# The light stage's loops over tiles, written out for every engine with constant waits and fixed addresses

## The chip, the cores and the metric

The kernel runs on one core of a Trainium2 chip. The metric is the device time of one execution in microseconds. A core has five engines with instruction streams of their own: TensorE (PE; its weight loads are listed apart as PEld), VectorE (DVE), ScalarE (ACT), GpSimd (POOL) and SyncE (SP). They meet through semaphores: an instruction adds to one when it is done, and another waits until it has reached a value.

## What is computed

Sixteen sequences of 512 tokens with 128 channels pass through a block of transformer layers: a feed-forward layer with routing, a latent attention, the same feed-forward layer again, an expert layer, a cosine attention and the expert layer again. The change lies in the light branch of the feed-forward layer, which runs twice. In the reference:

```python
def light_local_attn(x, gamma, wq, wkv, wo):
    xn = rmsnorm(x, gamma)
    q = xn @ wq
    k, v = jnp.split(xn @ wkv, 2, axis=-1)
    # windows of WIN = 128 tokens, HEADS = 8 heads of DH = 64
    q, k, v = (win(q) * SCALE, win(k), win(v))
    attn = jax.nn.softmax(jnp.einsum('bwhid,bwhjd->bwhij', q, k), axis=-1)
    out = jnp.einsum('bwhij,bwhjd->bwhid', attn, v)
    return out.transpose(0, 1, 3, 2, 4).reshape(b, n, HID) @ wo

def coor_descent(s, k):            # 50 rounds for the router, on scores of all tokens
    def body(_, ab):
        a, b = ab
        a = EPS * (logk - logsumexp((s + b) / EPS, axis=-1, keepdims=True))
        b = -relu(s + a)
        return (a, b)
    ...
```

The router then takes the 128 and the 256 tokens with the highest scores of each sequence (`top_k`).

## The kernel before

The 8192 tokens are 64 tiles of 128 tokens, one window each. `light_attention` (L346) runs them through a pipeline: five engines each have a `body(i, u, d, r)` that is called once for every pass i from -1 to 66. In pass i different tiles are at different steps. "Tile i" in this document means pass i. TensorE projects q and k of tile i (L507), does the output projection of tile i-3 (L514), transposes the probabilities of tile i-2 (L522), projects v (L527), transposes the input of tile i+1 (L532), makes the scores (L540) and multiplies probabilities and values of tile i-2 (L565). A pass begins with the first weight load of L507, and cuts are made there.

VectorE in a pass: row maxima `mx` of the scores (L653), the scores minus these, `ssub` (L657), half a round of the descent (`settle` L647, `descend` L641 and L642), `y` = the output plus the residual (L666), row sums `rsum` of the probabilities (L671), their reciprocals `rec` (L675), the normalised input of a later tile, `xr` (L632), and another half round. ScalarE: `oT` (L590), exponential `prob` (L595, needs `ssub`), `qkT` (L600), exponential and logarithm of the descent (L581, L583), `probT` (L606, twice), `v` (L609), `xrT` (L612) and the descent once more. GpSimd multiplies the probabilities by `rec` in two halves (L478). The order on an engine is the order in `body`, written by hand; nothing schedules it.

The passes 3 to 27 carry the descent (argument d), 28 to 59 the selection of the highest scores on VectorE (argument r; `max` L689, `match_replace` L692; `xr` is made on ScalarE there, L576), the others neither. `windows` (L416) calls `body` for the passes: -1 to 3 written out, 4 to 27 in a loop of six rounds of four passes (L421), 28 to 31 written out, 32 to 43 (L426) and 44 to 59 (L430) in loops of three and four rounds, 60 to 66 written out. `between(1)` and `between(2)` do work once after passes 43 and 59, on VectorE a mask of the selected tokens (L726, L729). In a loop, i is a register: a wait such as `dve.wait_ge(rec_ready, i)` compares with a register that has to be computed, and `x[:, bass.ds(j, 1), :]` is an address that has to be computed.

The stage is called with tag `f1l` (first call, 50 to 530 us of the span) and `f2l` (second call, from 1540 us).

Of the kernel before, what the change touches and what calls it, by code (L numbers as in the profile page):

```python
# [19 lines left out]
NT = TOK // P  # L20
# [325 lines left out]
def light_attention(nc, tag, x, y, scale_a, shift_b, s_rows, smax, na, logk, posw, wparts, lw, hw, w, ident, weff=None, consts=None):  # L346
# [5 lines left out]
    VB = 4  # L352
    wqkv, wo = lw["wqkv"], lw["wo"]
    with ExitStack() as ctx:
# [56 lines left out]
        D0 = 3  # L411
        D1 = D0 + ITERS // 2
        RQ, RKV = NQ // 8, NKV // 8
        E0 = D1 + RKV

        def windows(eng, body, between):  # L416


            for i in range(-1, VB):
                body(i, i % VB, 0 if i == D0 else None, None)  # L420
            with eng.Fori(1, D1 // VB) as k:  # L421
                for u in range(VB):
                    body(VB * k + u, u, 2 * (VB * k) + 2 * (u - D0) - 1, None)
            for i in range(D1, D1 + VB):
                body(i, i % VB, None, i - D1)
            with eng.Fori(D1 // VB + 1, (D1 + RQ) // VB) as k:  # L426
                for u in range(VB):
                    body(VB * k + u, u, None, VB * k + u - D1)
            between(1)
            with eng.Fori((D1 + RQ) // VB, E0 // VB) as k:  # L430
                for u in range(VB):
                    body(VB * k + u, u, None, VB * k + u - D1)
            between(2)
            for i in range(E0, NT + 3):
                body(i, i % VB, None, None)

        def live(i, lag=0):
            return not isinstance(i, int) or 0 <= i - lag < NT
# [27 lines left out]
        @block.gpsimd  # L466
        def _(pool):
            nc.gpsimd.memset(ones[:], 1.0).then_inc(filled, 1)
            if weff is not None:
                nc.gpsimd.memset(weff[:, 3:5], 0.0).then_inc(turned_clear, 1)  # L470

            def body(i, u, d, r):
                if live(i, 1):
                    pool.wait_ge(rec_ready, i)
                    pr, rc = prob[(u - 1) % 2], rec[(u - 1) % 2]
                    for n in range(2):
                        g = slice(PAIRS * n, PAIRS * n + PAIRS)
                        nc.gpsimd.tensor_tensor(pr[:, g], pr[:, g],  # L478
                                                rc[:, g].rearrange("p (h o) -> p h o", o=1).broadcast_to([P, PAIRS, P]),
                                                ALU.mult).then_inc(norm_ready, 1)  # L480

            def between(n):
                if n == 1:
                    pool.wait_ge(scores_ready, 1)
                    nc.gpsimd.tensor_scalar(one_minus[:], scores[:], -1.0, 1.0, ALU.mult, ALU.add).then_inc(less_ready, 1)
                    pool.wait_ge(less_ready, 1)
                    nc.gpsimd.tensor_tensor(weight[:], scores[:], one_minus[:], ALU.add).then_inc(weight_ready, 1)
                if n == 2:
                    pool.wait_ge(hw_in, 64)
                    kv = hraw[:, HID:3 * HID].rearrange("p (h s d) -> p s h d", h=HEADS, s=2)  # L490
                    nc.gpsimd.tensor_scalar(hw["wq"][:], hraw[:, 0:HID], hgamma[:, 0:1], None, ALU.mult)
                    nc.gpsimd.tensor_scalar(hw["wk"][:].rearrange("p (h d) -> p h d", h=HEADS), kv[:, 0], hgamma[:, 0:1], None, ALU.mult)
                    nc.gpsimd.tensor_scalar(hw["wv"][:].rearrange("p (h d) -> p h d", h=HEADS), kv[:, 1], hgamma[:, 0:1], None, ALU.mult)

            windows(pool, body, between)

        @block.tensor
        def _(pe):

            def body(i, u, d, r):  # L500
# [58 lines left out]
                if live(i, 2):  # L559
# [7 lines left out]
                    last.then_inc(o_ps, 1)  # L567

            windows(pe, body, lambda n: None)

        @block.scalar
        def _(act):
# [12 lines left out]
            def body(i, u, d, r):  # L585
# [35 lines left out]
                if at(i, NT + 2) and weff is not None:  # L621
                    act.wait_ge(weff_ps, 1)
                    nc.scalar.copy(weff[:, 0:3], ps_s[:, 0, 0:3]).then_inc(weff_sb, 1)

            windows(act, body, lambda n: None)

        @block.vector
# [2077 lines left out]
```

## Time and profile before

| what | value |
|---|---|
| median of three runs | 3093.97 us (3090.47 to 3094.25) |
| span of the profiled execution | 3097.8 us |
| busy share PE, DVE, ACT, POOL | 88%, 75%, 59%, 51% |
| tiles 4 to 27, first call / second call | 184.40 us / 187.58 us |
| tiles 32 to 59, first call / second call | 192.62 us / 192.72 us |

The span is the time from the first to the last instruction of one execution that was taken with the profiler; it lies 3.8 us above the median of the runs without it. The light stage is about 0.95 ms of it. The granted clock of TensorE is 1.00, its upper level of 2.4 GHz, over all tiles from 3 on in both calls. Register, branch and semaphore instructions are not counted as busy time, and the views do not list them: they show as idle time before the next instruction.

### The profile page before, as it was taken

How to read it: one execution, taken by the hardware profiler on the slowest of the kernel's cores; microseconds unless marked ns; L12 is line 12 of the kernel's file. 1: busy time of each engine (PE TensorE's matmuls, PEld its weight loads, DVE VectorE, ACT ScalarE, POOL GpSimd, SP SyncE). 2: the span in 40 equal slices, each digit the busy share in tenths (PEclk: the TensorE clock that was granted, in tenths of full speed). 3: DMA queues.
4: the chain of work that ended last, by engine and by line, in shares of the span. 5: the costliest groups of instructions: out<-in, count | busy, mean ns of one | idle time of the engine just before them, and what ended most of it. 6: DMA issues, size and time to landing. Idle time of an engine off the chain costs nothing. (4 is left out here: it accounts for less than half of the span.)

```text
span 3097.8 us, 73081 instructions
## 1 busy us (share of the span) xinstructions
PE 2738.8 (88%) x24470; PEld 1839.9 (59%) x24470; DVE 2312.9 (75%) x6119; ACT 1827.4 (59%) x3759; POOL 1587.2 (51%) x1866
## 2 busy tenths in 40 slices
PE   7989998999589999999788899989988469999795
PEld 4777887687223333333377788868766335555663
DVE  5898776788488888888388877779976357777563
ACT  3777665555246666666577766645553148876531
POOL 1222323787446666765322233377755646564446
PEclk9999999999779999999899999999988659999797
DMA  4000000000223333332000000000044365654343
GB/s 114 3 0 1 0 1 1 1 0 0 75 66 81 84 76 80 75 84 63 15 1 0 1 1 1 1 1 0 0 102 126 57 158 143 147 141 120 93 141 40
DMA packets 156192, 161.99 MB, mean 52 GB/s; under 512 B 42064, under 2 KB 134480, under 8 KB 155344
## 3 DMA queue, kind: packets, MB, share of 16 engines
q1 hardware_dynamic: 146624, 150.97, 19.3%
q0 software_dynamic: 9216, 7.87, 2.0%
q8 instruction: 113, 1.85, 0.3%
q14 instruction: 95, 0.78, 0.1%
q10 hardware_dynamic: 144, 0.52, 0.1%
HBM read 83.37 MB, written 74.87 MB: 51 GB/s over the span
## 5 line engine op out<-in xcount | busy, mean ns | idle before, releaser
L1969 DVE CUSTOM_DVE_ANT_0 la_ps<-la_ps,la_tri 128x512 f32<-128x512 f32 (+3 forms) x1024 | 481.8, 514 | 100.1 <-PE la_ps L1496 92.7
L1773 ACT ACTIVATE la_prob<-la_ps 128x512 f32<-128x512 f32 x640 | 373.8, 601 | 247.5 <-PE la_ps L1507 240.7
L478 POOL TENSOR_TENSOR f2l_prob<-f2l_prob,f2l_rec 128x512 f32<-128x512 f32 x128 | 133.1, 1060 | 330.8 <-DVE f2l_rec L675 330.8
L478 POOL TENSOR_TENSOR f1l_prob<-f1l_prob,f1l_rec 128x512 f32<-128x512 f32 x128 | 133.0, 1060 | 327.0 <-DVE f1l_rec L675 327.0
L1496 PE MATMUL la_ps<-la_ks,la_qs 48*128 48x512 bf16 (+3 forms) x1024 | 259.1, 321 | 45.0 <-DVE la_mx L1969 28.0
L1363 POOL TENSOR_SCALAR_AFFINE_SELECT la_prob<-la_prob 128x512 f32<-128x512 f32 x256 | 159.4, 634 | 217.6 <-ACT la_prob L1773 217.3
L1507 PE MATMUL la_ps<-la_qs,la_ks 50*128 50x512 bf16 (+3 forms) x1024 | 244.4, 310 | 5.8 <-ACT la_prob L1773 2.0
L1967 DVE TENSOR_REDUCE ca_mx<-ca_ps 128x4 f32<-128x512 f32 x256 | 174.2, 687 | 96.5 <-PE ca_ps L1496 95.5
L1507 PEld LDWEIGHTS la_ps<-la_qs,la_ks 50*128 50x128 bf16 x1024 | 67.0, 94 | 235.4 <-ACT la_prob L1773 162.9
L1773 ACT ACTIVATE ca_prob<-ca_ps 128x512 f32<-128x512 f32 x256 | 152.1, 602 | 89.4 <-PE ca_ps L1507 89.2
L1539 PE MATMUL la_ps_o<-la_prob,la_v 128*32 128x512 f32 (+3 forms) x2048 | 199.8, 464 | 0.0
L1969 DVE DVE_READ_ACCUMULATOR2_ANT la_mx<- 128x1 f32 x1024 | 144.6, 141 | 0.0
L1496 PEld LDWEIGHTS la_ps<-la_ks,la_qs 48*128 48x128 bf16 x1024 | 67.2, 95 | 113.7 <-DVE la_mx L1969 91.5
L507 PE MATMUL f2l_ps_qk<-f2l_xrT,fw_wqkv 128*128 128x128 f32 x1024 | 133.0, 284 | 0.7 <-ACT f2l_xrT L612 0.7
L507 PE MATMUL f1l_ps_qk<-f1l_xrT,fw_wqkv 128*128 128x128 f32 x1024 | 133.0, 284 | 0.7 <-ACT f1l_xrT L612 0.7
L507 PEld LDWEIGHTS f2l_ps_qk<-f2l_xrT,fw_wqkv 128*128 128x128 f32 x1024 | 120.7, 194 | 11.7 <-issue 10.5
L507 PEld LDWEIGHTS f1l_ps_qk<-f1l_xrT,fw_wqkv 128*128 128x128 f32 x1024 | 120.7, 194 | 11.7 <-issue 10.4
L595 ACT ACTIVATE f2l_prob<-f2l_ssub 128x1024 f32<-128x1024 f32 x64 | 67.8, 1059 | 85.2 <-DVE f2l_ssub L657 82.5
L595 ACT ACTIVATE f1l_prob<-f1l_ssub 128x1024 f32<-128x1024 f32 x64 | 67.7, 1059 | 79.5 <-DVE f1l_ssub L657 79.5
L1496 PE MATMUL ca_ps<-ca_ks,ca_qs 56*128 56x128 bf16 x1024 | 100.8, 228 | 10.7 <-DMA ca_ks<-stack_image 6.0
L1507 PE MATMUL ca_ps<-ca_qs,ca_ks 58*128 58x128 bf16 x1024 | 99.7, 224 | 3.2 <-ACT ca_prob L1773 1.9
L1507 PEld LDWEIGHTS ca_ps<-ca_qs,ca_ks 58*128 58x128 bf16 x1024 | 58.7, 96 | 69.4 <-ACT ca_prob L1773 35.6
(541 smaller groups left out, 8013.0 us busy)
## 6 DMA issues: line engine op xcount, KB each, us to landing
stack_image<-la_parts SPq DMA_DIRECT2D x192, 128.0 KB, 2.4
stack_image<-ca_parts SPq DMA_DIRECT2D x192, 128.0 KB, 2.4
la_qs<-stack_image SPq DMA_DIRECT2D x64, 192.0 KB, 3.5
la_ks<-stack_image SPq DMA_DIRECT2D x64, 192.0 KB, 4.3
ca_qs<-stack_image SPq DMA_DIRECT2D x64, 192.0 KB, 3.4
ca_ks<-stack_image SPq DMA_DIRECT2D x64, 192.0 KB, 4.3
gather_table<-fw_wqkv SPq DMA_DIRECT2D x16, 256.0 KB, 2.3
gather_table<-m_pr SPq DMA_DIRECT2D x32, 128.0 KB, 2.2
```

What stands on the lines that cost most here:

```text
L478: nc.gpsimd.tensor_tensor(pr[:, g], pr[:, g], rc[:, g].rearrange("p (h o) -> p h o", o=1).broadcast_to([P, PAIRS, P]), ALU.mult).then_inc( ...
L507: last = nc.tensor.matmul(ps_qk[:, t, p], wqkv[:, t, p * P:(p + 1) * P], xrT[:], start=True, stop=True)
L595: nc.scalar.activation(prob[(u - 1) % 2][:], ssub[:], ACT.Exp, scale=SM).then_inc(p_sb, 1)
L1363: return nc.gpsimd.affine_select(view, view, pattern=[[0, 4], [1, P]], compare_op=ALU.is_ge, fill=0.0, base=0, channel_multiplier=-1)
L1496: last = nc.tensor.matmul(bank[:, col:col + width], qs[u][rows, h // 2, qblk * P:(qblk + 1) * P], ks[u][rows, h // 2, keys], start=True, s ...
L1507: last = nc.tensor.matmul(bank[:, col:col + width], ks[u][rows, h // 2, blk * P:(blk + 1) * P], qs[u][rows, h // 2, blk * P:blk * P + widt ...
L1539: last = nc.tensor.matmul(ps_o[32 * j:32 * j + 32, blk * P:T], v[u][:, blk, 4 * q + j, :], prob[q % 2][:, unit, col:col + width], start=bl ...
L1773: nc.scalar.activation(prob[q % 2][:, n], ps2[n % 2][:], ACT.Exp, scale=SM).then_inc(S["p_sb"], 1)
L1967: last = nc.vector.tensor_reduce(m, bank[:].rearrange("p (a b) -> p a b", a=TPB), X_AX, ALU.max)
L1969: last = nc.vector.tensor_tensor_reduce(bank[:, col:col + width], bank[:, col:col + width], tri[:, T - width:T], 1.0, -BIG, ALU.add, ALU.m ...
```

## The change

`windows` no longer makes loops. It calls `body` with plain numbers for every pass, so that every wait has a constant and every address is fixed. The order of the calls, the arguments and the places of `between` are the same.

```diff
-            for i in range(-1, VB):
-                body(i, i % VB, 0 if i == D0 else None, None)
-            with eng.Fori(1, D1 // VB) as k:
-                for u in range(VB):
-                    body(VB * k + u, u, 2 * (VB * k) + 2 * (u - D0) - 1, None)
-            for i in range(D1, D1 + VB):
-                body(i, i % VB, None, i - D1)
-            with eng.Fori(D1 // VB + 1, (D1 + RQ) // VB) as k:
-                for u in range(VB):
-                    body(VB * k + u, u, None, VB * k + u - D1)
-            between(1)
-            with eng.Fori((D1 + RQ) // VB, E0 // VB) as k:
-                for u in range(VB):
-                    body(VB * k + u, u, None, VB * k + u - D1)
-            between(2)
-            for i in range(E0, NT + 3):
-                body(i, i % VB, None, None)
+            for i in range(-1, NT + 3):
+                descent = max(0, 2 * (i - D0) - 1) if D0 <= i < D1 else None
+                body(i, i % VB, descent, i - D1 if D1 <= i < E0 else None)
+                if i == D1 + RQ - 1:
+                    between(1)
+                if i == E0 - 1:
+                    between(2)
```

The built programs show it engine by engine. VectorE, second call, in the first loop, from the end of a half round of the descent to `xr`; ISA and REGISTER_ALU rows are register arithmetic for waits and addresses. Before:

```order
L664 ISA
L666 ISA x2
L666 SCALAR_TENSOR_TENSOR g_x<-f2l_ps_a,g_y 128x128
L670 ISA
L671 TENSOR_REDUCE f2l_rsum<-f2l_prob 128x8
L672 ISA
L674 ISA
L675 RECIPROCAL f2l_rec<-f2l_rsum 128x8
L677 ISA
L632 ISA x2
L632 REGISTER_ALU
L632 SCALAR_TENSOR_TENSOR f2l_xr<-g_y,g_a,g_b 128x128
```

After (the lines of the changed file are ten lower), with the instruction ahead of it:

```order
L632 TENSOR_SCALAR f2l_tmin<-f_s_rows,f_na 48x512
L656 SCALAR_TENSOR_TENSOR g_x<-f2l_ps_a,g_y 128x128
L661 TENSOR_REDUCE f2l_rsum<-f2l_prob 128x8
L665 RECIPROCAL f2l_rec<-f2l_rsum 128x8
L622 SCALAR_TENSOR_TENSOR f2l_xr<-g_y,g_a,g_b 128x128
```

The four working instructions keep their order, and the register rows between them are gone.

ScalarE, second call, in the first loop, around the exponential of the probabilities. Before:

```order
L583 ACTIVATE f2l_lsum<-f2l_esum 48x1
L587 REGISTER_ALU
L589 ISA
L590 COPY f2l_oT<-f2l_ps_v 128x512
L592 ISA
L594 ISA
L595 ACTIVATE f2l_prob<-f2l_ssub 128x1024
L597 ISA
L599 ISA
L600 COPY f2l_qkT<-f2l_ps_qk 128x1024
```

After:

```order
L573 ACTIVATE f2l_lsum<-f2l_esum 48x1
L580 COPY f2l_oT<-f2l_ps_v 128x512
L585 ACTIVATE f2l_prob<-f2l_ssub 128x1024
L590 COPY f2l_qkT<-f2l_ps_qk 128x1024
L571 ACTIVATE f2l_eexp,f2l_esum<-f2l_tmin,f2l_nm 48x512
```

Here too the register rows are gone and the working instructions stand as they stood.

## Rows read from the trace of the kernel before

**Rows 1.** Stretch, length, busy us of PE, PEld, DVE, ACT, POOL; clock, DMA share, GB/s.

```profile
75.47:82.31 6.84, 6.84 (x70) 5.82 (x68) 5.23 (x8) 5.05 (x10) 2.16 (x3) 1.00 0.15 34
82.31:266.71 184.40, 165.71 (x1610) 140.27 (x1609) 167.75 (x289) 143.56 (x310) 50.02 (x48) 1.00 0.00 0
295.78:488.40 192.62, 191.56 (x1878) 162.88 (x1876) 151.32 (x226) 127.91 (x224) 58.90 (x58) 1.00 0.00 1
1566.47:1754.05 187.58, 166.00 (x1611) 139.66 (x1609) 163.70 (x289) 145.35 (x310) 50.04 (x48) 1.00 0.00 0
```

**Rows 2.** Waits, 113 to 258 us: total us, times, longest.

```profile
ACT f1l_prob L595 <- DVE f1l_ssub L657: 16.8, 19, 1.0
PE f1l_ps_v L565 <- ACT f1l_v L609: 14.1, 18, 0.9
```

**Rows 3.** Timeline, tiles 13 to 15: start, us, instruction, [idle before and its releaser].

```profile
153.35 1.06 PE L514 MATMUL f1l_ps_a<-fw_wo,f1l_oT 128*128 128x128 f32 x8
...
154.58 0.29 DVE L666 SCALAR_TENSOR_TENSOR g_y<-f1l_ps_a,g_x 128x128 f32 x1 [0.27 <-PE f1l_ps_a L514]
...
156.14 0.20 DVE L675 RECIPROCAL f1l_rec<-f1l_rsum 128x8 f32<-128x8 f32 x1
...
156.42 2.08 POOL L478 TENSOR_TENSOR f1l_prob<-f1l_prob,f1l_rec 128x512 f32<-128x512 f32 x2 [5.67 <-DVE f1l_rec L675]
156.44 1.17 DVE L632 SCALAR_TENSOR_TENSOR f1l_xr<-g_x,g_a,g_b 128x128 f32 x1
...
159.95 1.23 DVE L657 TENSOR_TENSOR f1l_ssub<-f1l_ps_s,f1l_mx 128x1024 f32<-128x1024 f32 x1
...
161.29 1.06 ACT L595 ACTIVATE f1l_prob<-f1l_ssub 128x1024 f32<-128x1024 f32 x1 [0.96 <-DVE f1l_ssub L657]
...
165.78 1.09 PE L565 MATMUL f1l_ps_v<-f1l_probT,f1l_v 128*64 128x128 f32 x16 [0.84 <-ACT f1l_v L609]
...
169.92 0.29 DVE L666 SCALAR_TENSOR_TENSOR g_y<-f1l_ps_a,g_x 128x128 f32 x1 [0.26 <-PE f1l_ps_a L514]
```

**Rows 4.** Timeline, tile 3, outside the loops.

```profile
75.36 1.22 DVE L657 TENSOR_TENSOR f1l_ssub<-f1l_ps_s,f1l_mx 128x1024 f32<-128x1024 f32 x1
...
76.62 1.06 ACT L595 ACTIVATE f1l_prob<-f1l_ssub 128x1024 f32<-128x1024 f32 x1 [0.46 <-DVE f1l_ssub L657]
...
77.36 1.06 PE L514 MATMUL f1l_ps_a<-fw_wo,f1l_oT 128*128 128x128 f32 x8
...
78.45 0.29 DVE L666 SCALAR_TENSOR_TENSOR g_y<-f1l_ps_a,g_x 128x128 f32<-128x128 f32 x1 [1.36 <-PE f1l_ps_a L514]
...
79.91 0.20 DVE L675 RECIPROCAL f1l_rec<-f1l_rsum 128x8 f32<-128x8 f32 x1
...
80.19 2.08 POOL L478 TENSOR_TENSOR f1l_prob<-f1l_prob,f1l_rec 128x512 f32<-128x512 f32 x2 [4.64 <-DVE f1l_rec L675]
...
80.30 1.08 DVE L632 SCALAR_TENSOR_TENSOR f1l_xr<-g_x,g_a,g_b 128x128 f32<-128x128 f32 x1 [0.19 <-PE f1l_ps_a L532]
```

**Rows 5.** Timeline, second call, tile 13.

```profile
1640.17 0.29 DVE L666 SCALAR_TENSOR_TENSOR g_x<-f2l_ps_a,g_y 128x128 f32 x1
...
1641.87 0.20 DVE L675 RECIPROCAL f2l_rec<-f2l_rsum 128x8 f32<-128x8 f32 x1 [0.17 <-DVE f2l_rsum L671]
```

**Rows 6.** Timeline, tile 1, outside the loops.

```profile
67.61 0.30 DVE L632 SCALAR_TENSOR_TENSOR f1l_xr<-g_x,g_a,g_b 128x128 f32<-128x128 f32 x1
67.78 2.04 POOL L478 TENSOR_TENSOR f1l_prob<-f1l_prob,f1l_rec 128x512 f32<-128x512 f32 x2 [12.09 <-DVE f1l_rec L675]
```

**Rows 7.** Transfers of 113 to 258 and 488 to 525 us; fetch queue; a group of the first attention.

```profile
DMA packets 0, 0.00 MB, mean 0 GB/s; under 512 B 0, under 2 KB 0, under 8 KB 0
...
DMA packets 3, 0.04 MB, mean 1 GB/s; under 512 B 0, under 2 KB 0, under 8 KB 0
...
q8 instruction: 113, 1.85, 0.3%
...
L1969 DVE CUSTOM_DVE_ANT_0 la_ps<-la_ps,la_tri 128x512 f32<-128x512 f32 (+3 forms) x1024 | 481.8, 514 | 100.1 <-PE la_ps L1496 92.7 <-issue 0.2
```

## The prediction

> **What bounds the kernel now.** I read the light stage first in the table of busy time by stretch, cut at the places where TensorE's first weight load of a tile (L507) begins [rows 1]. Tile 3 still stands outside any loop: 6.84 us long, PE busy for all of it. So 6.84 us is what a tile costs when PE never waits. Tiles 32 to 59 (two of the three loops, 28 tiles) take 192.62 us, or 6.88 us each, with PE busy 191.56 us: PE is the bound there too, and shorter code on other engines can win little. Tiles 4 to 27 (the first loop, 24 tiles, with the descent of the router on DVE and ACT) are another matter: 184.40 us in the first call, 7.683 us a tile, and 187.58 us in the second, 7.816 us a tile, although the work is the same. PE is busy for 165.71 and 166.00 us of these, VectorE for 167.75 and 163.70 us, or at most 6.99 us a tile. No engine is full, so a chain of waits sets the pace, and the second call's extra 0.13 us is not arithmetic.
>
> The list of waits names the chain [rows 2]: PE waits for `v` from ACT before L565, ACT waits for `ssub` from DVE before the exponential. The third link is in the timeline, where DVE's `y` (L666) sits idle until PE's L514 releases it. There I followed the chain through two tiles [rows 3]: `y` at 154.58; `rec` at 156.14 (1.56 later); `ssub` of the next tile ends at 159.95 + 1.23 = 161.18 (5.04 later; GpSimd's multiply at 156.42 and `xr` at 156.44 lie inside); ACT's exponential starts 161.29 (0.11); PE's L565 starts 165.78 (4.49); DVE's `y`, two tiles on, starts 169.92 (4.14). Sum 15.34 us for two tiles, 7.67 each: this chain is the measured 7.683.
>
> **The change part by part.** Same instructions, same order. What goes is branches, and the register arithmetic that puts a wait value or an address before an instruction. It counts only where its instruction was about to start, which is three places in the chain. For each, tile 3, already written with constants, gives the price after [rows 4].
> - Before `y`: in the loop `y` starts 154.58, while L514 ended at 153.35 + 1.06 = 154.41, so 0.17 us. In tile 3 L514 ended at 77.36 + 1.06 = 78.42 and `y` starts at 78.45, so 0.03. Link 4.14 becomes 4.00.
> - Before `rec`: 1.56 from `y` in the loop, 79.91 - 78.45 = 1.46 in tile 3. Gain 0.10.
> - Before the exponential: 0.11 in the loop; in tile 3 `ssub` ends at 75.36 + 1.22 = 76.58 and the exponential starts at 76.62, so 0.04. Gain 0.07.
>
> I leave the links 5.04 and 4.49 alone. Register work inside them runs under long operations (ACT goes without a gap from the exponential to `v`), and `xr`, which also loses address arithmetic, is held by something else: in the loop it starts 0.02 us after GpSimd's multiply and takes 1.17 us [rows 3], in tile 3 it starts 0.11 after it and takes 1.08 [rows 4], and both end 1.19 us after GpSimd began. In tile 1, ahead of GpSimd, it took 0.30 us [rows 6]. Whoever comes second waits for the first multiply, so an earlier `xr` behind GpSimd ends no earlier.
>
> Sum after: 1.46 + 5.04 + 0.04 + 4.49 + 4.00 = 15.03 us for two tiles, 7.515 each. DVE alone would allow less (6.99 busy) and PE 6.84, so the chain still binds, only shorter. First call: 24 x (7.683 - 7.515) = 4.0 us. Second call: its loop is slower by more register work, `y` to `rec` takes 1641.87 - 1640.17 = 1.70 us instead of 1.56 [rows 5]. Written out both calls run the same form, so I take 7.515 there too: 24 x (7.816 - 7.515) = 7.2 us. The bounds: if the second call came down only to the first call's present 7.683, 24 x 0.133 = 3.2 us; if all of it goes, 7.2. I take 7.2, because the programs of the two calls read alike after the change.
>
> Tiles 32 to 59: 192.62 - 28 x 6.84 = 1.1 us above PE's own pace. That contains the mask at the middle, which stays. Bounds 0 and 1.1 us in a call; I take the middle, 0.5, since the mask costs VectorE part of it, so 1.0 us for both. Branches (13 loop rounds a call on four engines) lie in these measured means and get no price of their own. The straight tiles, the other stages and all transfers are not touched: 0.
>
> Total 4.0 + 7.2 + 1.0 = 12.2 us. The profiled execution has a span of 3097.8 us and gives 3085.6. The median of the shown runs is 3.8 us lower at 3093.97, so 3093.97 - 12.2 = 3081.8: **3082 us**.
>
> **Rivals.**
> A. *`xr` gets ahead of GpSimd.* In tile 3 `xr` was released by PE's L532 and came 0.11 us too late [rows 4]. If DVE runs a little later against PE, so that `rec` and with it GpSimd start over 0.11 later, `xr` goes first and takes 0.30 us [rows 6] where it ended 1.19 us after GpSimd's start. That takes some 0.8 us out of the link of 5.04: 14.2 us for two tiles, 7.1 each, a further 48 x 0.41 = 20 us, so 3062; with PE's 6.84 as a floor, 3050. Against it: two such chains run interlocked, one through the even tiles and one through the odd. Where `y` starts as soon as L514 ends, as in the chain's own pace, GpSimd wins as in tile 3. A tile in which `y` comes late can flip, but its neighbour then has `y` on time and stays at 15.03 for two tiles, and the mean stays 7.515 with tiles alternately long and short. So I expect flips in every other tile at most. The Trainium skill (SBUF — State Buffer, Who interferes with whom) says that a VectorE instruction with two SBUF inputs and a GpSimd instruction that reads SBUF exclude each other, and that issue order decides who blocks. The durations 0.30, 1.08 and 1.17 agree. By that rule a shift of 0.11 us in issue order would be worth this rival's whole 20 us.
> B. *Nothing measurable.* The three gains are eaten by the next wait: `rec` or `y` is early, but the last releaser (`v`, the probabilities, GpSimd) is late by other causes. Full loss of the gain gives 3094; half of it 3088. For it: idle DVE time is small (7.683 - 6.99 = 0.69 us a tile), so there is not much to squeeze. Against: each of the three gaps ends directly at a link of the chain that adds up to 7.67 of 7.683.
> C. *Slower: the written-out code has to be fetched.* During the first loop the instruction queues are silent: no packet at all in 145 us. In a straight stretch of 37 us (5.4 tiles) there are 3 packets; instruction queue q8 moved 113 in 0.3% of 16 engines' 3097.8 us, or about 1.3 us each [rows 7]. Estimated from this, 52 tiles a call that leave the loops cost 29 packets, 58 for both calls. Shown outright on the path each would be 1.3 us: 76 us, 3158. From 9 exposed packets the gain is gone, from 14 on it is measurably slower. Against it: tile 3 is straight code at PE's full pace, and the first attention runs DVE straight through 1024 pairs of instructions with 0.2 of 100.1 us idle put down to issue [rows 7], so fetching is ahead of use. The Trainium skill (Runtime: NRT & Kernel Launch, Instruction fetch mechanics) says that streaming is mostly hidden, but that a taken branch to a target outside the fetched window forces a fetch. The silent queue shows that these loops' branches cause none, so the removal of branches wins nothing by that rule.
> D. *The change does not do what it says*, and register work remains: the order of instructions shows none on DVE in these tiles after the change. I give it no chance of its own.
>
> **How the numbers follow.** Forecast (3077 to 3087): 0.60. A (3050 to 3077): 0.13. B (3087 to 3095): 0.19. C (over 3095): 0.08. About 0.2%, 6 us, is what a measurement of this kernel can tell from no change; 3094 - 6 = 3088 divides faster from same. So faster 0.74 (the edge of B with it), same 0.18, slower 0.08. The range takes in the forecast, A down to its two-tile value 3062 and B up to 3092, where half of the gain and more is lost; it leaves out A's floor and C: 3062 to 3092.
>
> **What would show it.** In the profile after: tiles 4 to 27 take 180.4 us (24 x 7.515) in both calls, perhaps alternating; the two calls agree, where they now differ by 3.2 us. `y` starts 0.03 us after L514's end, or after its own `tmin`; `rec` 1.46 after `y`; the exponential 0.04 after `ssub`; `xr` still takes 1.0 us or more in at least every other tile. Tiles 32 to 59 take about 192.1 us. The forecast is wrong if `xr` takes 0.3 us in all tiles (A), if tiles 4 to 27 stay above 7.65 us (B), or if gaps stand on PE, ACT or DVE that no releaser explains and that come along with packets of the instruction queues (C).

## The result, and the profile after

The median falls from 3093.81 us to 3072.97 us (five runs of each; 3068.53 to 3089.76 after, 3085.86 to 3094.25 before). The ratio is 0.9939, with an interval from 0.9915 to 0.9964. In microseconds that is 20.8 less, and anything from 11.1 to 26.3 less is inside the interval (3093.81 x 0.0036 and x 0.0085). The profiled execution after has a span of 3088.0 us, where before had 3097.8. The four stretches below are cut as in [rows 1], at TensorE's first weight load of a tile, now L497: tiles 4 to 27 and 32 to 59 of the first call, then the same of the second. Columns: stretch, length, busy us of PE, PEld, DVE, ACT, POOL (with counts), granted clock, DMA share, GB/s.

```profile
81.93:262.03 180.10, 165.66 (x1610) 140.66 (x1608) 153.33 (x289) 143.79 (x310) 51.86 (x48) 1.00 0.01 2
291.05:482.91 191.86, 191.47 (x1879) 162.86 (x1877) 149.15 (x226) 130.24 (x224) 59.12 (x59) 1.00 0.01 1
1565.95:1746.05 180.10, 165.65 (x1610) 140.65 (x1608) 153.48 (x290) 144.17 (x312) 52.05 (x48) 1.00 0.01 2
1775.06:1966.92 191.86, 191.47 (x1878) 162.85 (x1876) 148.80 (x226) 130.34 (x224) 59.11 (x59) 1.00 0.01 2
```

Against [rows 1] the first loop has lost 4.30 us in the first call and 7.48 us in the second. The two calls took 184.40 and 187.58 us; now both take 180.10. Tiles 32 to 59 have lost 0.76 us in the first call and 0.86 in the second (192.62 and 192.72 before). That is 13.4 us in all. Of the gain in tiles 32 to 59, 0.56 and 0.65 us lie in pass 44, the first one behind the mask of `between(1)`: it took 7.90 and 7.99 us and now takes 7.34 in both calls, while the passes around it take 6.83. TensorE's busy time in the stretches of [rows 1] is the same within 0.4 us, so what has gone is waiting.

The timeline shows the chain. These are rows of the passes 13 to 15 after (start us, us, engine, line, operation, in brackets the idle time before it and what ended it), in the part of the span that [rows 3] shows of before:

```profile
150.21 1.23 DVE L647 TENSOR_TENSOR f1l_ssub<-f1l_ps_s,f1l_mx 128x1024 f32<-128x1024 f32 x1
...
150.69 1.13 PE L504 MATMUL f1l_ps_a<-fw_wo,f1l_oT 128*128 128x128 f32 x8
...
151.47 1.06 ACT L585 ACTIVATE f1l_prob<-f1l_ssub 128x1024 f32<-128x1024 f32 x1 [0.87 <-DVE f1l_ssub L647]
...
152.24 0.28 DVE L656 SCALAR_TENSOR_TENSOR g_y<-f1l_ps_a,g_x 128x128 f32<-128x128 f32 x1
...
153.82 0.20 DVE L665 RECIPROCAL f1l_rec<-f1l_rsum 128x8 f32<-128x8 f32 x1
153.94 0.30 DVE L622 SCALAR_TENSOR_TENSOR f1l_xr<-g_x,g_a,g_b 128x128 f32<-128x128 f32 x1
...
154.10 2.26 POOL L468 TENSOR_TENSOR f1l_prob<-f1l_prob,f1l_rec 128x512 f32<-128x512 f32 x2 [5.34 <-DVE f1l_rec L665]
...
155.95 1.09 PE L555 MATMUL f1l_ps_v<-f1l_probT,f1l_v 128*64 128x128 f32 x16 [1.20 <-ACT f1l_v L599]
...
158.86 1.06 PE L504 MATMUL f1l_ps_a<-fw_wo,f1l_oT 128*128 128x128 f32 x8
...
159.96 0.29 DVE L656 SCALAR_TENSOR_TENSOR g_y<-f1l_ps_a,g_x 128x128 f32<-128x128 f32 x1 [1.23 <-PE f1l_ps_a L504]
...
161.41 0.20 DVE L665 RECIPROCAL f1l_rec<-f1l_rsum 128x8 f32<-128x8 f32 x1
...
161.69 2.08 POOL L468 TENSOR_TENSOR f1l_prob<-f1l_prob,f1l_rec 128x512 f32<-128x512 f32 x2 [5.33 <-DVE f1l_rec L665]
...
161.80 1.07 DVE L622 SCALAR_TENSOR_TENSOR f1l_xr<-g_x,g_a,g_b 128x128 f32<-128x128 f32 x1 [0.19 <-PE f1l_ps_a L522]
...
165.22 1.23 DVE L647 TENSOR_TENSOR f1l_ssub<-f1l_ps_s,f1l_mx 128x1024 f32<-128x1024 f32 x1
```

Two kinds of tile now take turns. In the even pass `y` (159.96) starts 0.04 us after L504 ends (158.86 + 1.06 = 159.92), having sat idle for 1.23 us. GpSimd begins at 161.69, and `xr` at 161.80 comes second and takes 1.07 us. In the odd pass VectorE is late: L504 had ended at 151.82, `y` starts at 152.24 with no idle time ahead of it, `xr` at 153.94 comes before GpSimd (154.10) and takes 0.30 us, as in [rows 6]; in tile 3 it had taken 1.08 [rows 4]. From pass 6 on the passes take 6.83 (even) and 8.17 us (odd) in turn; the mean over the 24 tiles is 7.504.

The chain of the forecast, now through the even `y`: to `rec` 161.41 - 159.96 = 1.45; to the end of the next `ssub` 166.45 - 161.41 = 5.04; from the end of an `ssub` (150.21 + 1.23 = 151.44) to the exponential 0.03; from there to L555 155.95 - 151.47 = 4.48; to `y` 159.96 - 155.95 = 4.01. The sum is 15.01 us for two tiles.

The groups of VectorE in tiles 4 to 27 of the first call show the turn of `xr` too (line, names, shapes, count; busy us, mean ns; idle before). Before, then after:

```profile
L642 DVE TENSOR_SCALAR f1l_tmin<-f_s_rows,f_na 48x512 f32<-48x512 f32 x48 | 29.5, 614 | 0.0
L632 DVE SCALAR_TENSOR_TENSOR f1l_xr<-g_x,g_a,g_b 128x128 f32 x24 | 28.3, 1179 | 2.1
```

```profile
L632 DVE TENSOR_SCALAR f1l_tmin<-f_s_rows,f_na 48x512 f32<-48x512 f32 x48 | 26.9, 560 | 0.0
L622 DVE SCALAR_TENSOR_TENSOR f1l_xr<-g_x,g_a,g_b 128x128 f32<-128x128 f32 x24 | 16.5, 689 | 2.3 <-PE f1l_ps_a L522 2.3
```

Mean 689 ns is the mean of twelve long and twelve short ones; it takes 11.8 us off VectorE's busy time, and most of the fall from 167.75 [rows 1] to 153.33 us is this. It is not the gain: behind a short `xr` VectorE waits the longer at `y` of the next pass (`y`'s idle time in these 24 tiles went from 4.6 us to 14.1).

The transfers of the same 145 us as in [rows 7], where before had no packet, and the two instruction queues over the whole execution (name, packets, MB, share of 16 engines):

```profile
DMA packets 15, 0.20 MB, mean 1 GB/s; under 512 B 0, under 2 KB 0, under 8 KB 0
```

```profile
q8 instruction: 157, 2.57, 0.4%
q14 instruction: 111, 0.91, 0.1%
```

The written-out code is fetched: 44 packets more on q8 (113 in [rows 7]) and 16 more on q14, which had 95. No gap on the path goes with them: the short passes take 6.83 us, as tile 3 did (6.84 [rows 1]), and the links above add up to the length of two passes.

### The profile page after: what moved, and what is told of

Its sections match the earlier page's. It is cut to its first block and busy times, and to the rows that moved or that the text cites. A ratio compares the mean times of both kernels' runs of the same rounds, so it can differ in the third digit from the quotient of the medians.

```text
span 3088.0 us, 70516 instructions
## 1 busy us (share of the span) xinstructions
PE 2732.6 (88%) x24470; PEld 1834.5 (59%) x24470; DVE 2276.8 (74%) x6119; ACT 1829.0 (59%) x3759; POOL 1592.3 (52%) x1866
## 5 line engine op out<-in xcount | busy, mean ns | idle before, releaser
L497 PE MATMUL f2l_ps_qk<-f2l_xrT,fw_wqkv 128*128 128x128 f32 x1024 | 133.0, 284 | 0.7 <-ACT f2l_xrT L602 0.7
L497 PE MATMUL f1l_ps_qk<-f1l_xrT,fw_wqkv 128*128 128x128 f32 x1024 | 133.0, 284 | 0.7 <-ACT f1l_xrT L602 0.7
L497 PEld LDWEIGHTS f1l_ps_qk<-f1l_xrT,fw_wqkv 128*128 128x128 f32 x1024 | 120.7, 194 | 11.7 <-issue 10.4
L497 PEld LDWEIGHTS f2l_ps_qk<-f2l_xrT,fw_wqkv 128*128 128x128 f32 x1024 | 120.7, 194 | 11.7 <-issue 10.5
```

Source lines behind the costliest of these rows:

```text
L497: last = nc.tensor.matmul(ps_qk[:, t, p], wqkv[:, t, p * P:(p + 1) * P], xrT[:], start=True, stop=True)
```

## The experiments

The theory: the time came from register work at links of one chain of waits, most of it on VectorE, and the meeting of `xr` with GpSimd holds what is left at 7.5 us a tile. Its rivals: another loop or engine gave it, or another wait holds the rest. e2, e3, e4, e6 and e7 were executed once each, so their stretches are read and not their times.

**The changed kernel again (e1_again).** The 13.4 us seen in the light stage are less than the 20.8 us of the medians, so the first question is whether either number repeats. No edit.

> The changed kernel once more. Its profile showed the light stage 13.4 us shorter (tiles 4 to 27: 180.1 us in both calls instead of 184.4 and 187.6; tiles 32 to 59: 191.9 instead of 192.6 and 192.7), while the medians differed by 20.8 us. Theory 1: the light stage gives 13.4 us in every execution and the rest is the granted clock of TensorE in the other stages, which differs from execution to execution; then the light stage is the same to 0.2 us in this profile, the ratio is near 0.9957 and spans go with the mean clock. Theory 2: the written-out code also shortens later stages by some 6 us every time; then the ratio is again near 0.994 and some later stage is shorter in this profile too.

Measured: 3076.17 us (ten runs) against 3098.53 (fifteen), ratio 0.9937, interval 0.9909 to 0.9964. Tiles 4 to 27 take 180.11 and 180.10 us, tiles 32 to 59 191.86 in both calls. The light stage repeats to 0.01 us. The medians differ by 22.4 us this time, and the interval again reaches down to 11.2. So the light stage repeats, but the ratio came out where theory 2 had put it and not at theory 1's 0.9957; the last three runs come back to this.

**The first loop alone (e2_first_loop).** Which of the three loops carries the gain? The kernel before, with only this:

```diff
-            with eng.Fori(1, D1 // VB) as k:
-                for u in range(VB):
-                    body(VB * k + u, u, 2 * (VB * k) + 2 * (u - D0) - 1, None)
+            for i in range(VB, D1):
+                body(i, i % VB, 2 * (i - D0) - 1, None)
```

> The kernel before with its first loop alone (tiles 4 to 27) written out. Theory (the chain over two tiles loses its register work): 180.1 us for tiles 4 to 27 in both calls, 192.6 us for tiles 32 to 59 as before, the light stage 11.7 us shorter. Rival (the gain needs all loops gone, or comes from branches between loops): less than 6 us.

Tiles 4 to 27 of both calls (columns as in the first table):

```profile
81.62:261.71 180.09, 165.66 (x1610) 140.67 (x1608) 153.35 (x290) 144.18 (x312) 52.12 (x48) 1.00 0.01 2
1560.58:1740.68 180.10, 165.68 (x1610) 140.57 (x1608) 156.35 (x289) 143.32 (x310) 51.33 (x48) 1.00 0.01 1
```

The whole gain of tiles 4 to 27 is there. Tiles 32 to 59 stay at 192.72 and 193.16 us, so their 0.8 us a call belong to the other two loops. From pass 22 of the second call on, `xr` here comes behind GpSimd in every pass (1.08 to 1.13 us) and the passes take 7.4 and 7.6 us instead of 6.83 and 8.17; two of them still make 15.0 us, and the stretch is as long as in the first call. For the pace it makes no difference whether `xr` comes second in every pass or in every other one; every other one is enough to hold the chain.

**Engine by engine (e3_dve_only, e4_all_but_dve).** The forecast put two of its three links on VectorE and one on ScalarE. In the first kernel only VectorE gets the written-out form, in the second only the other three engines; `written` is `windows` of the changed kernel, and each kernel has both functions.

```diff
-            windows(dve, body, between)
+            written(dve, body, between)
```

```diff
-            windows(pool, body, between)
+            written(pool, body, between)
...
-            windows(pe, body, lambda n: None)
+            written(pe, body, lambda n: None)
...
-            windows(act, body, lambda n: None)
+            written(act, body, lambda n: None)
```

> Only VectorE's passes written out, the other engines keep loops. Theory (VectorE's register work ahead of y and rec is 0.24 of the 0.31 us per two tiles in the first call): tiles 4 to 27 take 181.2 us (7.55 a tile) in the first call and 181.2 to 183 in the second. Rival (the gain comes from branches and register work on all engines alike): 183 us or more in the first, 185 or more in the second.

> VectorE keeps its loops, the other engines are written out. Theory: only the 0.07 us ahead of the exponential goes, so tiles 4 to 27 take 183.5 us in the first call (7.65 a tile) and about 186.5 in the second. Rival (all engines alike): 182 and 183 us or less.

Tiles 4 to 27, VectorE alone written out:

```profile
82.81:264.05 181.24, 165.94 (x1610) 140.74 (x1608) 153.10 (x289) 144.53 (x310) 51.89 (x48) 1.00 0.00 0
1557.53:1738.38 180.85, 167.35 (x1611) 140.39 (x1609) 153.47 (x290) 146.03 (x312) 52.11 (x48) 1.00 0.00 0
```

And all but VectorE:

```profile
81.38:264.61 183.23, 165.71 (x1611) 140.29 (x1609) 167.51 (x289) 142.15 (x310) 50.07 (x48) 1.00 0.01 1
1555.05:1741.91 186.86, 165.96 (x1610) 140.34 (x1608) 163.49 (x289) 142.32 (x310) 50.07 (x48) 1.00 0.01 1
```

VectorE's loop is worth 3.16 us in the first call and 6.73 in the second, the other three engines' loops 1.17 and 0.72. The parts add up to 4.33 and 7.45 us, where all together gave 4.30 and 7.48. So the gains are links of one chain, one behind the other, and the second call's extra is VectorE's. VectorE's busy time tells the same: 153 us (`xr` short in every other tile) only where VectorE is written out. With VectorE alone written out the second call, at 180.85 us, lies a little under the 181.2 to 183 expected. Tiles 32 to 59 follow VectorE too: 191.94 and 191.87 us with VectorE alone written out, 192.46 and 192.67 with the others.

No run parts the branches of the loops from their register arithmetic; every written-out form drops both. The rows of before bound it for the first call: the chain in [rows 3] lies inside one round (passes 12 to 15), crosses no branch and takes 15.34 us, where the mean of the loop is 15.37. That leaves an estimated 0.3 of the 4.30 us for the branches.

Why the second call had more to lose is in the program before. The same source became, in the first loop of the first call, from `tmin` to `xr`:

```
L642 TENSOR_SCALAR f1l_tmin<-f_s_rows,f_na 48x512
L666 ISA
L666 SCALAR_TENSOR_TENSOR g_y<-f1l_ps_a,g_x 128x128
L671 TENSOR_REDUCE f1l_rsum<-f1l_prob 128x8
L674 ISA
L675 RECIPROCAL f1l_rec<-f1l_rsum 128x8
L677 REGISTER_ALU
L632 ISA
L632 SCALAR_TENSOR_TENSOR f1l_xr<-g_x,g_a,g_b 128x128
```

That is four register instructions; the piece of the second call that is shown with the change has ten from before `y` to `xr`. Over the 24 tiles the trace of before holds 161 register operations on VectorE in the first call and 412 in the second.

**`xr` on ScalarE (e5_xr_on_act, e6_loops_xr_on_act).** If the meeting of `xr` and GpSimd is what holds the chain at 7.5 us, `xr` on another engine must let it go. From pass 28 on both kernels make `xr` on ScalarE already; e5 does it from pass 3 on in the changed kernel, e6 in the kernel before, with its loops.

```diff
         def late(i, r):
-            return r is not None or isinstance(i, int) and i >= D1
+            return r is not None or isinstance(i, int) and i >= D0
```

```diff
         def late(i, r):
-            return r is not None or isinstance(i, int) and i >= D1
+            return r is not None or not isinstance(i, int) or i >= D0
```

> The changed kernel with xr made by ScalarE from tile 3 on (one bound in the helper that decides it, 3 instead of 28), so that VectorE no longer meets GpSimd at xr. Theory (in the tiles with y on time, xr held by GpSimd's first multiply is the slow piece of the two-tile chain): about 1.0 us leaves the link from rec to ssub, 14.0 us for two tiles, 7.0 a tile, near TensorE's own 6.84; tiles 4 to 27 take 164 to 169 us, both calls together 22 to 32 us shorter than with the change alone. Rival (ScalarE, which lies in the same chain, pays for xr): 0.53 us more a tile, no gain, 180 us or more.

> The kernel before, loops kept, with xr made by ScalarE from tile 3 on. Theory: the same piece goes from the chain with its register work, 15.34 - 1.0 = 14.3 us for two tiles in the first call, 7.2 a tile, 172 us; second call 175. If TensorE's 6.84 were already the bound in both forms, written out or not would no longer matter and this kernel would equal the written-out one with xr on ScalarE.

Tiles 4 to 27 of e5, then of e6:

```profile
81.80:249.38 167.58, 165.07 (x1610) 140.14 (x1608) 144.73 (x265) 149.56 (x335) 53.20 (x48) 1.00 0.01 2
...
1553.89:1721.48 167.59, 165.09 (x1610) 140.16 (x1608) 144.98 (x265) 149.57 (x335) 53.19 (x48) 1.00 0.01 2
```

```profile
82.29:254.06 171.77, 165.13 (x1610) 140.05 (x1608) 143.68 (x265) 151.52 (x334) 52.94 (x48) 1.00 0.00 0
1562.94:1737.07 174.13, 165.70 (x1610) 139.58 (x1608) 144.90 (x265) 152.29 (x335) 53.27 (x48) 1.00 0.00 0
```

6.98 us a tile, with TensorE busy for 165.07 of 167.58 us: PE is now nearly the bound here too. The median is 3051.9 us (six runs) against 3092.61 (eleven) of the kernel before, ratio 0.985, interval 0.9813 to 0.9886; the changed kernel was not run beside it, but its fastest run of all took 3066.93 us, the slowest here 3065.43. In the first call the two effects stand side by side. Moving `xr` is worth 12.52 us there with written-out code (180.10 - 167.58) and 12.63 with loops (184.40 - 171.77). Writing the loops out is worth 4.19 and 6.54 us where `xr` is out of the way, against 4.30 and 7.48. In the second call they overlap by 0.9 us: with loops the move is worth 13.45 us there, and it also takes `xr`'s own register rows off VectorE (316 are left of 412).

**GpSimd behind `xr` (e7_xr_first).** Rival A said that `xr` ahead of GpSimd in every tile gives 7.1 us a tile. Here GpSimd is made to wait for it, with `xr` still on VectorE:

```diff
                     pool.wait_ge(rec_ready, i)
+                    if D0 <= i < D1:
+                        pool.wait_ge(xr_ready, i + 3)
```

> The changed kernel in which GpSimd's multiply of tiles 3 to 27 also waits for xr of the same tile, one more wait on GpSimd, so that xr goes first in every tile. Theory (issue order at xr decides, not the amount of work): xr takes 0.30 us in all tiles, tiles 4 to 27 about 7.2 each, 173 us in both calls, and the alternation of 6.83 and 8.17 disappears. Rival (the alternation has another cause, and GpSimd's later start costs the transposes of the next tile): 180 us or more.

Tiles 4 to 27, and one meeting of the two (lines of this kernel are two higher):

```profile
82.01:256.81 174.80, 165.70 (x1610) 140.26 (x1608) 154.89 (x289) 142.61 (x311) 53.66 (x49) 1.00 0.01 2
1555.93:1730.74 174.81, 165.71 (x1610) 140.26 (x1609) 155.01 (x289) 142.60 (x311) 53.66 (x49) 1.00 0.01 2
```

```profile
151.83 0.20 DVE L667 RECIPROCAL f1l_rec<-f1l_rsum 128x8 f32<-128x8 f32 x1
...
152.22 0.35 DVE L624 SCALAR_TENSOR_TENSOR f1l_xr<-g_x,g_a,g_b 128x128 f32<-128x128 f32 x1 [0.19 <-PE f1l_ps_a L524]
...
152.72 2.22 POOL L470 TENSOR_TENSOR f1l_prob<-f1l_prob,f1l_rec 128x512 f32<-128x512 f32 x2 [4.90 <-DVE f1l_xr L624]
```

The wait costs GpSimd 0.6 us (it starts 0.89 us after `rec`, where the even pass above had 0.28), and still the tile falls from 7.504 to 7.283 us. The order of the two alone, with no work taken away, is worth 5.3 us a call. The alternation was expected to go and only shrank, to 7.11 and 7.45 us.

**Where is the rest of the medians' 20.8 us? (e8_before_a, e9_before_b, e10_after_c)** Two profiles of the kernel before and one of the changed kernel, on one chip, to compare what lies outside the light stage.

> The kernel before, unchanged, to see what the stages outside the light stage do from one execution to the next. Theory 1 (the light stage gave 13.4 us, what the medians show above that is drift of the other stages with TensorE's granted clock): the span less the two light stages lies between 2124 and 2150 us, as in the eight profiles so far, and those of the kernel before are not longer as a group; tiles 4 to 27 take 184.4 and 187.6 us again. Rival (the change also shortens something outside the light stage by some 6 us): the kernel before lies at 2136 us or above each time.

> The kernel before once more, the same expectation: theory 1, 2124 to 2150 us outside the light stages with no order by kernel; the rival, 2136 us or above.

> The changed kernel once more: theory 1, 2124 to 2150 us outside the light stages, tiles 4 to 27 at 180.1 us in both calls; the rival, some 6 us less outside them than the two runs of the kernel before beside it.

The spans are 3097.8, 3110.2 and 3078.3 us. Tiles 4 to 27 take 184.40 and 187.57, 184.39 and 187.56, 180.14 and 180.13 us. The span less the two light stages (from their first instruction to the first of the heavy attention) is 2138.4, 2149.8 and 2131.7 us. With the earlier profiles that is 2138 to 2150 for before (three) and 2129 to 2141 for after (three). So before is longer as a group, which theory 1 had excluded, and it lies above 2136 us each time, as the rival said: by these six alone the rival, some 6 us outside the light stage, would stand. But kernels with loops reach both ends of the whole range: e4 2124.3, e6 2149.9. And the largest of these stages, the first attention, moves with TensorE's granted clock. The stretch is cut here where its first and the next stage's first instruction start: the second profile of before, then e4, which runs the same code there.

```profile
796.60:1550.90 754.30, 682.64 (x4896) 245.58 (x4896) 582.71 (x2365) 441.89 (x819) 451.97 (x621) 0.88 0.29 70
```

```profile
791.00:1521.30 730.30, 658.07 (x4896) 238.88 (x4896) 582.02 (x2365) 441.68 (x820) 452.75 (x622) 0.91 0.30 72
```

The same 4896 matmuls take PE 24.6 us more at a mean granted clock of 0.88 than at 0.91, and the stretch is 24.0 us longer; the other engines' work is the same within 1 us. The first profile of before had 737.5 us here, so one kernel alone varies by 17 us between executions. Over all twelve profiles of the study (all 12 cut this way) the length of this stretch follows the time that the clock stood at its lower level, 1.2 GHz, in it, from 126 to 188 us: a straight line of 0.39 us per us, correlation 0.97, with no residual over 3.2 us (before -0.1, 1.2 and 0.7; after -3.2, -2.9 and 1.2). So the stages outside drift by more than the difference in question, and neither kernel lies wholly on one side of the line.

The granted clock of single executions takes this further; it is on record for 29 executions of the kernel before and 16 of the changed kernel. Their means differ by 19.8 us. Two straight lines of time against clock, one for each kernel and with the same slope, fall by 2.3 us per 0.001 of clock and lie 13.2 us apart, with a 95% interval from 10.6 to 15.7 (12.4 us if the time at the lower level is taken in place of the clock). So at the same clock the changed kernel is shorter by what the light stage gave, 13.4 us, and there is no room for 6 us more. The rest goes with the clock, which was 0.9271 on average in the changed kernel and 0.9242 before. Theory 1 stands in this form. Why the changed kernel's executions had the higher clock is open; written-out code alone does not bring it, for the six runs of e5 had 0.9232.

## Why the prediction was right

- **The direction and the place.** The forecast was 3082 us with a range from 3062 to 3092; 3072.97 is inside it and faster by more than 0.2%. The gain that rows show is in tiles 4 to 27 and 32 to 59, apart from 0.2 and 0.4 us in pass 60, the first one behind the last loop (7.56 and 7.72 us before, 7.33 after).
- **The chain.** Forecast 1.46 + 5.04 + 0.04 + 4.49 + 4.00 = 15.03 us for two tiles; measured 1.45 + 5.04 + 0.03 + 4.48 + 4.01 = 15.01. The static prices of tile 3 [rows 4] held link by link, also the two links left alone.
- **First and second call.** 4.0 us expected, 4.30 measured; 7.2 expected, 7.48 measured. Both calls now take the same time, as forecast from the programs reading alike.
- **Tiles 32 to 59.** 0.5 us a call as the middle of 0 and 1.1; 0.76 and 0.86 measured. The middle was a guess; 0.5 us stay, in pass 44 behind the mask (7.34 against 6.83), where the guess left 0.6.
- **The total.** 12.2 us against 13.4 in the light stage, and 20.8 by the medians. What the forecast did not price is that other stages drift from execution to execution by more than its whole sum. Its point, 3082, misses the median by 9 us: 1.2 us of that are the light stage, and nearly all of the rest goes with the clock of the executions, as the comparison at one clock shows. That the median lies in the range is partly luck. 3072.97 is below the band of 3077 to 3087 that had the chance of 0.60 and in the band of rival A, for which the low end of the range was drawn and which did not come.
- **Rival A** did not come by itself: `xr` flipped in every other tile, the mean stayed at 7.50, and the tiles alternate, which is what the text said. That the even `y` waits and the odd does not was its reason, and the timeline shows it. Its mechanism is real, as e7 and e5 show. Its condition, a shift of 0.11 us, was read too small, as rows of before show (pass 16):

```profile
179.41 1.22 DVE L632 SCALAR_TENSOR_TENSOR f1l_xr<-g_x,g_a,g_b 128x128 f32 x1
...
179.43 2.08 POOL L478 TENSOR_TENSOR f1l_prob<-f1l_prob,f1l_rec 128x512 f32<-128x512 f32 x2 [5.59 <-DVE f1l_rec L675]
```

By its record `xr` starts 0.02 us ahead here and still takes 1.22 us; it takes 0.30 at 0.16 us ahead (153.94 against 154.10 after). From tile 3's place the flip needs somewhere between 0.13 and 0.27 us. The forecast's 7.1 us a tile was a little too good for the wait (7.28) and not good enough for the move to ScalarE (6.98).
- **Rival B** fails: no other wait took the 4.3 and 7.5 us. e3 and e4 add up, so nothing of it was lost between links.
- **Rival C**: 58 packets estimated, 60 counted, none on the path. The Trainium skill (Runtime: NRT & Kernel Launch, Instruction fetch mechanics) says that streaming is mostly hidden; 15 packets in 145 us in which every even pass ran at PE's pace, 6.83 us, agree. It also says that taken branches are one reason to unroll. Here they cost no fetch (no packet in the 145 us before [rows 7]), and what unrolling took away was register work in the main.

## What to carry to other kernels

Register arithmetic ahead of a wait or an address was free here where its instruction was no link of the chain that sets the pace (passes 37 to 43 take 6.83 or 6.84 us with loops and without); on the chain it cost 0.07 to 0.14 us per place, once in every two tiles, and the price can be read from a tile of the same work that stands outside the loop. Follow the chain over as many tiles as it spans, here two, before summing. And before a small gain is looked for in the whole time, compare the stage's own stretch in several profiles: 13.4 us repeated to 0.1 us there, while the stages that were not touched moved by up to 26 in sum.

## What the hardware did that was not expected

- One source, called twice, gave programs with 161 and 412 register operations on VectorE in the same 24 tiles, and VectorE's loop cost 3.2 us in the one and 6.7 in the other.
- The meeting with GpSimd is not only `xr`'s. With `xr` gone from VectorE (e5), `tmin`, with one input from SBUF, takes 1.01 or 0.91 us while GpSimd multiplies and 0.47 us otherwise:

```profile
149.48 2.22 POOL L468 TENSOR_TENSOR f1l_prob<-f1l_prob,f1l_rec 128x512 f32<-128x512 f32 x2 [4.89 <-DVE f1l_rec L665]
...
149.78 1.01 DVE L632 TENSOR_SCALAR f1l_tmin<-f_s_rows,f_na 48x512 f32<-48x512 f32 x1
...
153.60 0.47 DVE L632 TENSOR_SCALAR f1l_tmin<-f_s_rows,f_na 48x512 f32<-48x512 f32 x1
```

The Trainium skill (SBUF — State Buffer, Who interferes with whom) says that `tensor_scalar` can run in a mode that takes the port pair it shares with GpSimd, and that whoever comes first blocks the other. The durations agree; no row shows the mode. So the move of `xr` handed part of the wait to the next long instruction: `tmin`'s mean rose from 560 to 709 ns. In e7 the `tmin` behind GpSimd's start takes 1.05 us in the same way.
